# Attention block on one core: another opening, another place for the attention read-back, a projection tile by tile, and x of the last batch in free tiles

## The reference, cut to what matters

```python
xn = groupnorm(x) * gn_w + gn_b
qkv = einsum('oc,bct->bot', qkv_w, xn) + qkv_b          # per head 64 q, 64 k, 64 v
weight = softmax(einsum('bct,bcs->bts', q, k) / sqrt(64))
a = einsum('bts,bcs->bct', weight, v)
out = xn + einsum('oc,bct->bot', proj_w, a) + proj_b
```

## Time and profile before

| | |
|---|---|
| median of 3 runs | 3774.83 us (3774.66 to 3775.08) |
| the profiled execution, its time | 3774.18 us |
| its span, first to last instruction | 3772.5 us |
| mean granted TensorE clock | 0.997 |
| TensorE busy | 3699.3 us (98%) |
| GpSimd, ScalarE, VectorE busy | 3001.7, 2867.9, 2246.3 us (80%, 76%, 60%) |
| chain that ended last, by engine | PE 91%, ACT 3%, DMA 2%, DVE 2% |

### The profile page before, as it was taken

How to read it: one execution, slowest core, us unless ns; L and a number is a source line. 1 busy time by engine, 2 the same in 40 slices (tenths; PEclk the granted TensorE clock), 3 DMA queues, 4 the chain that set the end, 5 groups by cost and what they waited for, 6 DMA issues and landing times.

```text
span 3772.5 us, 74528 instructions
## 1 busy us (share of the span) xinstructions
PE 3699.3 (98%) x30004; PEld 2263.6 (60%) x30004; DVE 2246.3 (60%) x2820; ACT 2867.9 (76%) x4037; POOL 3001.7 (80%) x1639
## 2 busy tenths in 40 slices
PE   6999999999999999999999999999999999999998
PEld 4565565655856556565675656556567565656556
DVE  4566557656555565765646565666655656565653
ACT  2777777787577777778757777777876777777885
POOL 0788888888388888888838888888874888888994
PEclk9999999999999999999999999999999999999999
DMA  2000012011400001201140000110223000000014
GB/s 80 14 23 22 21 36 69 23 56 38 146 21 19 24 23 32 73 19 58 44 139 19 23 23 17 52 53 27 68 63 104 23 21 21 22 19 19 20 37 138
DMA packets 133673, 165.02 MB, mean 44 GB/s; under 512 B 61648, under 2 KB 110800, under 8 KB 132816
## 3 DMA queue, kind: packets, MB, share of 16 engines
q1 hardware_dynamic: 133328, 160.26, 13.5%
HBM read 122.17 MB, written 38.04 MB: 42 GB/s over the span
## 4 chain that ended last, share of the span: by engine, by line
PE 91%; ACT 3%; DMA 2%; DVE 2%; issue 1%; SPq 1%; POOL 0%; POOLq 0%; ACTq 0%; DVEq 0%
PE oacc L611 29%; PE scores L590 23%; PE pool_bank L538 13%; PE aux_banks L560 12%; PE pool_bank L550 7%; PE scores L690 4%; PE pool_bank L577 1%; ACT probs L795 1%; ACT scores L808 1%; DVE maxima L911 1%; DMA out<-probs 1%; PE scores L538 1%; DMA neg_rows<-neg_cols 1%; POOL denom L1157 0%; DVE o_norm L1018 0%
## 5 line engine op out<-in xcount | busy, mean ns | idle before, releaser
L1157 POOL TENSOR_TENSOR denom<-denom,probs 128x768 f32<-128x768 f32 x1536 | 2825.5, 1840 | 425.0 <-ACT probs L795 235.0
L911 DVE TENSOR_REDUCE maxima<-aux_banks 128x2 f32<-128x512 f32 x1728 | 1656.0, 958 | 1314.9 <-PE aux_banks L560 1281.9
L795 ACT ACTIVATE probs<-scores 128x768 f32<-128x768 f32 x1728 | 1311.2, 812 | 676.1 <-PE scores L590 668.1
L808 ACT ACTIVATE scores<-seeds 128x768 f32<-128x768 f32 x1728 | 1342.6, 823 | 19.3 <-PE scores L598 10.0
L611 PE MATMUL oacc<-probs,vals 128*64 128x384 f32 x6912 | 1283.0, 492 | 0.0
L611 PEld LDWEIGHTS oacc<-probs,vals 128*64 128x64 f32 x6912 | 455.0, 136 | 523.3 <-issue 381.9
L560 PE MATMUL aux_banks<-k_hi,q_hi 64*128 64x512 f32 (+1 forms) x3456 | 684.0, 391 | 20.7 <-DVE maxima L911 18.8
L560 PEld LDWEIGHTS aux_banks<-k_hi,q_hi 64*128 64x128 f32 x3456 | 322.8, 183 | 548.9 <-issue 443.8
L590 PE MATMUL scores<-q_hi,k_hi 64*128 64x384 f32 x3456 | 599.6, 343 | 17.3 <-ACT scores L808 17.0
L590 PE MATMUL scores<-q_lo,k_hi 64*128 64x384 f32 x3456 | 587.6, 335 | 0.0
L590 PE MATMUL scores<-q_hi,k_lo 64*128 64x384 f32 x3456 | 587.5, 335 | 0.0
(11 more groups left out here) (91 smaller groups left out, 1476.4 us busy)
## 6 DMA issues: line engine op xcount, KB each, us to landing
seeds<-neg_rows SPq DMA_DIRECT2D x96, 384.0 KB, 3.5
xtile<-x SPq DMA_DIRECT2D x72, 384.0 KB, 3.2
att<-o_norm SPq DMA_DIRECT2D x96, 192.0 KB, 1.9
probs<-x SPq DMA_DIRECT2D x24, 768.0 KB, 4.5
out<-probs SPq DMA_DIRECT2D x24, 768.0 KB, 3.7
xtile<-att SPq DMA_DIRECT2D x12, 768.0 KB, 4.6
att_raw<-att SPq DMA_DIRECT2D x12, 768.0 KB, 6.3
neg_rows<-neg_cols SPq DMA_DIRECT2D x384, 0.8 KB
```

What stands on the lines that cost most here:

```text
L795: a(prob(s).rearrange("p (h n) -> p h n", n=N), scores[:, s % 2, :, 0:N], ACT.Exp, scale=SCALE).then_inc(probs_ready, 1)
L808: a(scores[:, s % 2, :, 0:N], seeds[blk % 2][:, :].rearrange("p (e n) -> p e n", n=N), ACT.Copy).then_inc(seeded, 1)
L911: v.tensor_reduce(maxima[:, :, qt, kc], aux_banks[:, :, 0:UNIT_KEYS[kc % 2]], AX.X, ALU.max)\
L1157: gp.tensor_tensor(acc, acc, prob(s), ALU.add).then_inc(added, 1)
```

## The change

**Opening.** The first channel tile of x is loaded in three parts. TensorE runs 40 matmuls of 128 columns on the mask tile before the sums and 10 after the second group matmul (`keep_busy`). The 32 bias passes are gone: the v bias is now added to the attention tiles when they are split (high part: Identity with a bias; low part: scalar_tensor_tensor), one operation for each 128 channels instead of one for all four. The 12 normalizing operations are split, channel tiles 0 and 1 on ScalarE, 2 and 3 on VectorE (`SHARE`). After k0, q0, k1 each unit is followed by two quarters of a preparation. The exponential's table is loaded early. The seeds of block 0 go out ahead of wv's load, and wproj_lo is made on VectorE after the 18th unit's maximum.

**Stream.** `STATS_STEPS` skips the steps at which a block ends. The read-back of the first two attention tiles stands two steps later, at `READ_STEP`.

**Projection.** Each tile gets its 12 matmuls in one piece.

**Last batch.** x comes in four loads into `xn`, four steps after `READ_STEP`; the sum is made there, and the last four tiles are stored one by one.

```diff
-    STATS_AT, STATS_EVERY = 30, 2
+    STATS_AT, STATS_EVERY = 28, 2
+    SHARE = 2
...
+        between = (quarters("k", 2, 3) + quarters("v", 0) + quarters("k", 4, 5) + quarters("v", 1) +
+                   quarters("q", *range(1, EARLY_Q)) + quarters("v", *range(2, VG)))
+        units = [("aux", qt, kc) for kc in range(CH) for qt in range(QT)]
+        units += [("aux", u // CH, u % CH) for u in range(QT * CH, AHEAD)]
...
+        for n, key in enumerate(units):
+            order.append((key, 0, PARTS))
+            order += between[2 * n:2 * n + 2]
...
+        READ_STEP = 2 + next(s for s, blk in PUT_AT.items() if blk == BLOCKS - 4)
-        STATS_STEPS = {STATS_S0 + STATS_AT + STATS_EVERY * n: n for n in range(XITEMS)}
+        STATS_STEPS = {s: n for n, s in zip(range(XITEMS), (
+            s for s in range(STATS_S0 + STATS_AT, LAST_S0, STATS_EVERY) if s not in PUT_AT))}
...
+                    if last and s == READ_STEP + 4:
+                        wait_full(sp, use(b, last, ("q", PAIRS - 1, CH - 1)))
+                        for k in range(CT):
+                            sp.dma_start(xn[:, k, :], x[b, k * 128:(k + 1) * 128, :]).then_inc(xlast_in, 16)
+                    if s == READ_STEP:
+                        sp.wait_ge(xn_ready, scaled(b if last else b + 1))
+                        sp.wait_ge(att_out, PRIMED + 16 * (BLOCKS * (b + 1) - 3))
+                        load_att(b, 0)
+                        load_att(b, 1)
...
+                    if last and tc == CH - 1:
+                        for ot in range(CT):
+                            sp.wait_ge(out_ready, PRIMED + PJ * b + CT * tc + ot + 1)
+                            sp.dma_start(out[b, ot * 128:(ot + 1) * 128, chunk(tc)],
+                                         residual(tc, last)[:, ot, :]).then_inc(out_last, 16)
+                        continue
...
+                    pe.wait_ge(att_hi_ready, CT * (CH * b + tc + 1))
+                    pe.wait_ge(att_lo_ready, CT * (CH * b + tc + 1))
+                    for ot in range(CT):
+                        n = tc * CT + ot
+                        if n >= 4:
+                            pe.wait_ge(proj_saved, PRIMED + PJ * b + n - 3)
+                        for w, a in ((wproj_hi, att_hi[i]), (wproj_lo, att_hi[i]), (wproj_hi, att_lo[i])):
...
+            def keep_busy(n):
+                for _ in range(n):
+                    mm(aux_banks[:, 0, 0:128], groups[:, :], groups[:, :], start=True, stop=True)
...
+            def tiles_made(part):
+                pe.wait_ge(xn_ready, SHARE * (part + 1))
+                pe.wait_ge(xn_first, (CT - SHARE) * (part + 1))
...
+                for k in range(rows.start, rows.stop):
+                    a(att_hi[i][:, k, :], att_raw[i][:, k, :], ACT.Identity, bias=bvs[:, k:k + 1])\
+                        .then_inc(att_hi_ready, 1)
...
+                    v.scalar_tensor_tensor(att_lo[i][:, k, :], att_raw[i][:, k, :], bvs[:, k:k + 1],
+                                           att_hi[i][:, k, :].bitcast(fp32), ALU.add, ALU.subtract)\
+                        .then_inc(att_lo_ready, 1)
```

More of the change, by code:

```diff
@@ L257, in xres, with residual @@
             return probs[:, CT * N * (2 + i):CT * N * (3 + i)].rearrange("p (o n) -> p o n", n=N)
+        def residual(tc, last):
+            return xn[:, :, chunk(tc)] if last else xres(tc % 2)
         def four(buf):
@@ L463, in chan, with projection @@
                 return ap[bass.ds(b, 1), :, chunk(tc)].rearrange("b (k c) t -> c (b k) t", c=128)
-            def projection(b):
-                sp.wait_ge(pv_done, PRIMED + BSTEPS * (b + 1))
-                sp.wait_ge(added, PRIMED + ADDS * BLOCKS * (b + 1))
-                for tc in range(2):
-                    sp.dma_start(xres(tc), chan(x, b, tc)).then_inc(xres_in[tc], 16)
+            def projection(b, last):
+                if not last:
+                    sp.wait_ge(pv_done, PRIMED + BSTEPS * (b + 1))
+                    sp.wait_ge(added, PRIMED + ADDS * BLOCKS * (b + 1))
+                    for tc in range(2):
+                        sp.dma_start(xres(tc), chan(x, b, tc)).then_inc(xres_in[tc], 16)
                 for tc in range(CH):
@@ L477, in projection @@
                         put_block(b, BLOCKS - 1)
+                    if last and tc == CH - 1:
[4 more added lines that the diff above has]
+                        continue
                     sp.wait_ge(out_ready, PRIMED + PJ * b + CT * (tc + 1))
[L479 to L480 removed]
+                    sp.dma_start(chan(out, b, tc), residual(tc, last)).then_inc(stored[i], 16)
+                    if tc + 2 < CH and not last:
                         sp.wait_ge(stored[i], PRIMED + 16 * (CH // 2 * b + tc // 2 + 1))
@@ L505, in batch @@
                 stream(b, last)
-                projection(b)
+                projection(b, last)
             for b in range(B):
@@ L698, in _ @@
             units = 0
-            for key in FIRST:
+            keep_busy(40)
+            for key, since, until in FIRST_ITEMS:
                 kind, i, j = key
@@ L1023, in att_low @@
                 dve.wait_ge(att_hi_ready, CT * (CH * b + tc) + rows.stop)
-                v.tensor_tensor(att_lo[i][:, rows, :], att_raw[i][:, rows, :], att_hi[i][:, rows, :].bitcast(fp32),
-                                ALU.subtract).then_inc(att_lo_ready, rows.stop - rows.start)
+                for k in range(rows.start, rows.stop):
+                    v.scalar_tensor_tensor(att_lo[i][:, k, :], att_raw[i][:, k, :], bvs[:, k:k + 1],
+                                           att_hi[i][:, k, :].bitcast(fp32), ALU.add, ALU.subtract)\
+                        .then_inc(att_lo_ready, 1)
             def unit_of_step(s, b, last):
```

158 lines of the change are left out of this document (80 added, 78 removed).

## The result

The changed kernel takes **3740.8 us** (median of four runs, 3740.33 to 3741.51); the kernel before took 3774.95 beside it (3774.66 to 3776.40). The ratio is 0.9907, 95% interval 0.9896 to 0.9919. It gained 34.2 us where 41.5 was forecast. The forecast time was 3733.3, and the result lies 0.3 us above the upper end of the range. The profiled execution took 3741.51 us, with a span of 3739.7.

The account below looks back on a forecast made before the run. Inside the stream only TensorE time or waits of TensorE were taken to count, with most idle time in the opening. Gains of 23.8 + 1.6 + 2.4 + 6.5 + 7.2 = 41.5 off 3774.8 gave 3733.3 us, range 3728.5 to 3740.5.

Parts of the forecast that it names:

- Term 1, the opening: Opening: the unit that started at 101.74 us would start at 77.9, a gain of 23.8 us.
- Start: Start of the opening: loading x's first tile in three is worth 0.5 us; first group matmul 19.1, k0 at 24.95.
- Warm-up: Opening, before the sums: 80 passes of the 40 matmuls take 8.7 to 17.4 us, ending at 10.7 to 19.4.
- the first rival: Opening: warm-up passes outlast the sums or k0 starts at the lower clock; 2 to 6 us later, 3738; chance 0.12.
- Units: Opening's score units: quarters of preparations fill the gaps; 1.64 us per 256 unit, 1.76 per 512, 42.0 in all.
- Term 2: Projection tile by tile: low parts cost nothing, with 3.3 us margin; shorter seed wait at three batch borders gains 1.6 us.
- the "slower" rival: Projection: TensorE waits for slow low parts at 5 groups per batch; 3787 us if 2.7 late each; chance 0.02.
- Term 3: Sums of x: skipping one step per batch but the last removes a 0.8 us TensorE wait three times, 2.4 us.
- Term 4: Read-back behind the maxima: seeds no longer come late; 3 x 0.78 + 2.6 + 1.6 = 6.5 us.
- what fell with the wait stays away with it: Last batch, within the read-back term: the clock's fall behind the seed wait goes too, half of 3.3 us.
- Term 5, the end: Last tiles: early x, no late attention tile and a 192 KB last store end the span at 3765.3, gaining 7.2 us.
- Only the ends gain, the waits move: Whole kernel: the waits of terms 2 to 4 move to the next late operation; gain 31.0, 3743.8 us; chance 0.07.

Follow-up runs that it names:

- Experiment 1: The changed kernel with the first tile of x loaded in one piece of 1152 KB again, as in the kernel before: 3739.97 us.
- experiment 4: The changed kernel with the sums of x at the steps of the kernel before, also where o_norm is made: 3742.97 us.
- the fifth experiment: The changed kernel with the two read-back loads of attention ahead of the maxima on SyncE's queue again, in all four batches: 3742.18 us.
- 8: The changed kernel with TensorE instead of GpSimd making the last denominator addition of the last batch's third last and second last blocks: 3738.51 us.
- 9: The changed kernel with those two additions on TensorE and also the read-back ahead of the maxima, as in the kernel before: 3744.17 us.
- second: The changed kernel without the 40 warm-up matmuls ahead of the sums; the ten behind them stay: 3742.79 us.
- third: The changed kernel without the ten warm-up matmuls behind the sums; the 40 ahead stay: 3744.63 us.
- eleventh: The changed kernel with the projection's second tile's high and low parts made early, into free k buffers, in the last batch: 3740.03 us.
- tenth: The changed kernel with GpSimd leaving out the last six additions of the last batch's last block: 3739.49 us.

## Why the prediction was right or wrong

**Faster by more than 0.2%, with 0.97:** right. **41.5 us:** 7.5 too much in the times.

**Term 1, the opening: 23.8 forecast, 20.9 measured.**
- *Start.* This step failed. The forecast had the sums at 19.1, with a gain of 0.5 from thirds of the first tile; they were ready at 20.57. I took the landing time of every tile from a trace in which each load had 1152 KB, and let the first tile alone change. Experiment 1 shows the price, 0.9 us; with the 0.5 that was never there this is the whole delay of the sums, 1.5. k0 came 1.7 late.
- *Warm-up.* 80 passes took 10.89 us, the lower bound that I had chosen was 8.7, and they ended at 12.92, clear of the sums. k0 ran at full clock, so the first rival did not come in by this way in the profiled execution. That is in part luck: of the eleven traces that keep both warm-ups, five have the clock rise only after k0 had begun (k0 2.86 to 3.33 us).
- *VectorE's TENSOR_SCALAR* took 0.60 us each (six in 3.62, one by itself 0.67), below the bound of 1.0. The estimate of 0.5 that rested on the Trainium skill (VectorE: DVE Perf Modes, the perf-mode tier table) was a little low. It changed nothing, as said.
- *Preparations.* 7.97 us against 8.2.
- *Units.* The mechanism was right: quarters filled the gaps, and TensorE had no idle time over 0.2 us from 35 to 69. The pace was a little slower, 1.75 us for the small kind and 1.88 for the large (1.64 and 1.76 forecast). The 24 units took 43.4 us from the end of the preparations instead of 42.0, although the wait for wproj_lo was 1.31 and not 2.0. Two quarters took 1.44 us, not 1.37.
- *Handover.* 2.7 from the last unit to the stream's second, 2.8 forecast.
- *A term left out.* The kernel before ran the first steps of its stream at the lower level. That went too, 0.6 us, so up to the tenth exponential the changed kernel gained 21.5.

**Term 2: 1.6 forecast.** The wait at the border went from 1.11 to 0.75, and by place each border gave 0.48: 1.4. But "margin 3.3 us: cost nothing" was wrong once. In the last batch GpSimd is still adding when the projection starts, the low parts take 8.3 us instead of 2.2, and TensorE waited 2.44. This is the mechanism of the "slower" rival, at one group in twenty. I had seen its sign in the earlier trace rows (3.14 us for an operation that should take less) and set it aside with "GpSimd has nothing to add in most of the projection". That holds for three batches; in the fourth GpSimd ends its additions 10.4 us into the projection (3692.55, start 3682.1).

**Term 3: 2.4 forecast, 1.8 to 2.2 measured** (experiment 4). "Next late" was a maximum two slots earlier, 0.29 a batch.

**Term 4: 6.5 forecast.** In the first three batches the read-back gave 2.8 us by place (changed kernel against the fifth experiment, from exponential 264 to 400 of each), 2.3 forecast. In the last batch the same comparison gives 4.5 us up to exponential 400, forecast 4.2. Then it was lost again. GpSimd adds without a pause from 3496 to 3692 (1.97 us an addition, 17 a block, 33.5 us, where nine slots of 3.2 us take 28.8 at the end of the batch). Its place does not move when TensorE gets ahead, so TensorE meets it later: 3.51 us at 3655, and a fall of the granted clock behind it that lasts 6.8 us where the old one lasted 3.4. The failed step is "what fell with the wait stays away with it". I looked only at the queue in front of the wait and not at what was about to become the bound behind it; the square of experiments 5, 8 and 9 shows that it was GpSimd.

The loss has two parts. GpSimd ended its additions 30.5 us earlier than before (3692.55 against 3723.07), TensorE stood 34.95 ahead at exponential 400, so some 4.4 of that had to come back if it was to end no closer to GpSimd than before. The rest, 2.4, goes with the fall of the clock: TensorE ended up only 28.1 ahead. How long the fall lasts varies from trace to trace. Behind the same wait of 3.5 us it was 6.8 us here, in the second, third and eleventh experiments, and 3.4 in the first, fourth and tenth, whose 31 exponentials took 56.6 to 56.8 us instead of 57.28. The first, fourth and eleventh experiments also show once more that GpSimd's place is what holds. Their traces lack a wait of 1.42 us for a maximum that the changed kernel's has at 3509.82, and each waits 0.7 to 0.8 us for a denominator at 3625 to 3628 (0.39 at 3624.86 in the changed kernel):

```profile
3625.16 0.87 PE L612 MATMUL pool_bank<-denom,ones 128*64 128x384 f32 x4 [0.73 <-POOL denom L1219]
```

**Term 5, the end: 7.2 forecast, 7.1 measured.** From the last exponential to the end of the span the two traces differ by 32.8 - 28.1 = 4.7 us, and 2.4 of wait stand against that. The last store closed the span 3.1 us after the save, as the sum had it (0.6 + 1.9 + 0.6).

**The rivals.** None came out as stated. "Only the ends gain, the waits move" was right in the last batch alone, and there the wait moved to an engine that I had not named.

**Still open:** why the runs without a warm-up are 1.2 to 1.5 us slower than their openings explain, and some 0.7 us that the changed kernel gained in the first half of the last batch without a named cause. Both are near the spread of single runs.

## What to carry to other kernels

Before you book a removed wait as a gain, look for the engine that has been busy without a pause up to there: its place does not move, and what is won ahead of it comes back as a wait for it. A helper engine with a share of the work that is right on average can still be the bound in the last stage, where the others have less to do. And before you put a fraction of a microsecond down to an edit, look in several traces whether the clock fell somewhere by itself. Splitting a transfer helps only if the consumer of the first piece is the bottleneck; ask what it does to the loads behind it.

## What the runs showed of the hardware

- VectorE operations with two SBUF operands (low parts of attention, residual adds) take about one GpSimd addition each when four stand in a row while GpSimd adds: 2.07 against 0.55 us for 384 columns. A single one between other work took anything from 0.55 to 2.22 (o_norm in the last 200 us of the changed kernel). One with an operand in PSUM took 0.61 beside running additions.
- A tile of 1152 KB in three loads was complete 0.9 us later than in one, and the three tiles behind it came 1.5 us later.
- The granted clock fell to 0.50 at 15.85, in the 7.65 us in which TensorE had nothing to do behind the 80 passes, and rose at 26.09, with the 20 passes from 22.32 on in between. Without these, k0 ran at 0.50 and took 4.16 us instead of 2.80 (2.80 to 3.33 in the eleven traces that have them and the 80).
